# A two-stage convolution and scan kernel on one core: who adds up the sixteen units of the first level

## The chip, the cores and the metric

The kernel runs on one core of a Trainium2 chip. The metric is the device time of one execution in microseconds, where lower is better. A core has five engines with queues of their own: TensorE (PE in the profile; PEld is its weight load), VectorE (DVE), ScalarE (ACT), GpSimd (POOL) and SyncE (SP), which here issues every DMA. They meet only in semaphores. All data of the part in question are float32.

## The reference, cut to what matters

An input of 16 images with 256 channels of 32x32 goes through two residual blocks, each behind a group normalization. The first block computes 7x7 depthwise filters from the image and convolves the image with them. The second is a state-space scan over three levels of resolution (1024, 256 and 64 positions), in two directions:

```python
def _ssm(x, xw, dtw, dtb, Al, Dv, g, be):
    ...
    def step(h, inp):
        da, dbx, c = inp
        h = h * da + dbx
        return (h, jnp.einsum('bdn,bn->bd', h, c))
    ...
    y = ys.transpose(1, 0, 2) + xt * Dv
    return _layernorm(y, g, be)
```

So for each of 16 states n there is a scan over the positions, its result is multiplied by the row C[n], and the 16 products are summed. At the first level (1024 positions) this is done once forward and once backward. The sum plus x times D goes through a layer norm over the 128 channels, the two directions are added, and the result is gated, projected and added to the image.

## The kernel before

The 128 inner channels lie on the partitions, the positions along the free dimension. The scan of one image is cut into 37 *units* (`UNITS`): unit 0 is level 3, units 1 to 4 are level 2 (four states each, both directions), units 5 to 20 are the sixteen states of level 1 forward, and units 21 to 36 the sixteen of level 1 backward. A *product* (`PRODUCTS`) is one unit in one direction, so q = k + 5 for the units of level 1. For a unit k of level 1:

- SP fetches the broadcast rows B[n] into `bb` (two buffers, `get_b`) and C[n] into `cb` (three, `get_c`), 512 KB each. `get_b(k)` waits until `bx` of unit k-2 is made, `get_c(k)` until the products of unit k-3 are.
- GpSimd makes `bx` = `bb` * `u` (`inputs`, L1315; it needs the scan of unit k-2 done, since `bx` has two buffers). I call it bx(k).
- ScalarE makes the decay exp(delta * A[n]) in PSUM, `slot_b`, in two halves (`decay`, L1173), each after the scan of unit k-1 in the same half.
- VectorE scans each half (`scan`, L552) from `slot_b` and `bx` into PSUM, `slot_c`, the second half starting from the first one's last element, and multiplies each half by `cb` into SBUF, `h`, one of three buffers (`weigh`, L561). `products` orders this as: first scan of k, second multiply of k-1, second scan of k, first multiply of k. I call the start of a unit's first scan S(k).
- GpSimd adds the product `h` to the running sum `y` (`gather`, L1343). I call it y(k). Its program order is bx(k+1), y(k-1), bx(k+2), y(k), and so on, one unit ahead with the inputs and one behind with the sums.

The layer norm (`norm_centre` and `norm_spread` on TensorE, `norm_square` and `norm_root` on ScalarE, `norm` on VectorE) is done in six pieces (`NORMS`): 0 and 1 are levels 3 and 2, 2 and 3 the two halves of the forward direction, 4 and 5 those of the backward one. `norm_centre` multiplies `y` by the 128x128 matrix `cen`, which takes the mean over channels away.

Everything is software-pipelined over images. One *body* runs the 37 units of image i, the convolution of image i+1 (98 taps of six matmul instructions each; `taps`, L790), and the preparation of image i+2, interleaved by hand tables (`ROOM`, `pre`, `NORM_*`, `CHUNK_*`). TensorE's taps need `diag` matrices, which ScalarE makes between the decays (L1059). After unit 36 comes the *bridge*: it ends the norm and the output of image i (norms 4 and 5, `output`) and starts the scan of image i+1. A full body is run 14 times in a `Fori` loop; a body without preparation and one without taps end the program.

Other places that the prediction names: the first-level rows of B, C and delta are computed in *chunks* of 512 positions (`chunk` on TensorE, L831 and L832; `chunk_exp`, `chunk_log` on ScalarE; `chunk_first`, L500, and `chunk_last`, L508 and L510, on VectorE; `chunk_low` on GpSimd). Chunks 4 and 5 (backward direction) are done around units 13 to 16; chunk 4 starts on TensorE when norm 1 has ended on VectorE (L588). VectorE also adds the convolution to the image at units 10 and 33 (`conv_add`, L486); the second of these releases the statistics, the new weights and the rest of the body's end on ScalarE. VectorE's other small pieces of preparation (`pre`) lie at units 17 to 27, norms 2 and 3 at units 30 and 33. The buffer `ob` holds the output image from the bridge until its DMA has left, counted by `ob_free`.

Of the kernel before, what the change touches and what calls it, by code (L numbers as in the profile page):

```python
# [5 lines left out]
ALU = mybir.AluOpType  # L6
# [28 lines left out]
UNITS = [(3, 2, 2, 0, NS)] + [(2, 1, 2, n, 4) for n in range(0, NS, 4)] + \  # L35
# [3 lines left out]
PRODUCTS = [(u, d) for u, (_, _, dd, _, _) in enumerate(UNITS) for d in ((0, 1) if dd == 2 else (dd,))]  # L39
NP = len(PRODUCTS)  # L40
# [6 lines left out]
HR = 3  # L47
BR, CR = 2, 3
# [13 lines left out]
def banks(q):  # L62

    u, d = PRODUCTS[q]
    return (1, 0) if UNITS[u][0] == 1 and d else (0, 1)
# [7 lines left out]
def half_at(q, p):  # L73
    return 2 * (q - 2) + p
# [10 lines left out]

def weighed(q):
    return q + 1 if q < 2 else 2 * q


NHALF = 2 * (NP - 2)  # L90
# [3 lines left out]
def build(nc, a, bc, out):  # L94
    with ExitStack() as ctx:
        def sb(name, shape, dt=F32):
            return ctx.enter_context(nc.sbuf_tensor(name, shape, dt))

        def ps(name, shape, dt=F32):
            return ctx.enter_context(nc.psum_tensor(name, shape, dt))  # L100
# [32 lines left out]
        ident, cen, ones, grp, grp_m2, halves, halves_m2 = (mats[n] for n in CONSTS)  # L133
# [59 lines left out]
        u = sb("u", [P, LS])  # L193
        y = sb("y", [P, 2, LF])
        bb = sb("bb", [P, BR, HW])
        cb = sb("cb", [P, CR, HW])
# [11 lines left out]
        ob = sb("ob", [P, CT, HW])  # L208
# [3 lines left out]
        slot_c = ps("slot_c", [P, HW])  # L212
# [8 lines left out]
        ob_free = Count("ob_free", 16)  # L221
# [75 lines left out]
        q_h3 = Count("q_h3", 2)  # L297
        q_h = Count("q_h", NHALF)
        q_pr = Count("q_pr", weighed(NP - 1))
        q_y = Count("q_y", NP)  # L300
        n_y = Count("n_y", 24)
        n_yc = Count("n_yc", NN)
        n_sq = Count("n_sq", NN)
# [21 lines left out]
        def bank(t, k):  # L325
            return t[:, k * HALF:(k + 1) * HALF]

        def norm_psum(k):

            t = {4: slot_b, 5: slot_c}.get(k, pm)  # L330
            return bank(t, 0), bank(t, 1)
# [10 lines left out]
        def half(ap, b):  # L342
            return ap[:, b * HALF:(b + 1) * HALF]
# [5 lines left out]
        def _(sp):  # L349
# [29 lines left out]
            def get_c(i, k):  # L379
                if k >= CR:  # L380
                    sp.wait_ge(q_pr.sem, q_pr.at(i, weighed(products_of(k - CR)[-1])))
                get_rows(i, k, NS, cb[:, k % CR, :], c_in[k % CR])
# [34 lines left out]
        def _(dve):  # L417
# [137 lines left out]
            def weigh(i, q, p):  # L555
                k, b = PRODUCTS[q][0], banks(q)[p]
                dve.wait_ge(c_in[k % CR].sem, c_in[k % CR].at(i, 16 * (k // CR + 1)))
                dve.wait_ge(q_h.sem, q_h.at(i, half_at(q, p) + 1))
                if p == 0 and q >= HR:
                    dve.wait_ge(q_y.sem, q_y.at(i, q - HR + 1))  # L560
                nc.vector.tensor_tensor(half(h[:, q % HR], b), bank(slot_c, b), half(cb[:, k % CR], b), ALU.mult).then_inc(q_pr.sem, 1)  # L561

            def products(i, k):

                if k == 0:
                    weigh_least(i, 0)
                    weigh_least(i, 1)
                    return
                late = halves_of(k - 1)[-1] if k > 1 else None
                for q, p in halves_of(k):  # L570
                    same = late is not None and banks(late[0])[late[1]] == banks(q)[p]
                    if same:
                        weigh(i, *late)
                    scan(i, q, p)
                    if late is not None and not same:
                        weigh(i, *late)
                    late = q, p
                if k == NU - 1:
                    weigh(i, *late)
# [99 lines left out]
        def _(pe):  # L679
# [154 lines left out]
            def norm_centre(i, k):  # L834
                d, c0, n = NORMS[k]
                src = y[:, :, c0:c0 + n] if d == 2 else y[:, d, c0:c0 + n]
                cols = 2 * n if d == 2 else n
                if k == 0:
                    pe.wait_ge(y_init.sem, y_init.at(i, 5))
                elif k < 4:  # L840
                    pe.wait_ge(n_o.sem, n_o.at(i, STEPS[k]))
                pe.wait_ge(q_y.sem, q_y.at(i, NORM_NEEDS[k]))
                o = norm_psum(k)[0][:, 0:cols]
                if d == 2:
                    o = o.rearrange("p (d n) -> p d n", d=2)
                nc.tensor.matmul(o, cen[:, :], src, start=True, stop=True).then_inc(n_yc.sem, 1)  # L846

            def norm_spread(i, k):
                d, c0, n = NORMS[k]
# [10 lines left out]
            def bridge(i, j, m):  # L860
                def some(lo, hi):
                    if m is not None:
                        taps(m, BRIDGE_TAPS[lo], BRIDGE_TAPS[hi])
                some(2, 3)
                if j is not None:
                    lower(j, 0)
                some(3, 4)
                if j is not None:
                    lower(j, 1)
                some(4, 5)  # L870
                if j is not None:
                    chunk(j, 0)
                if i is not None:
                    norm_centre(i, 4)
                    norm_centre(i, 5)
                if j is not None:
                    chunk(j, 1)
                if i is not None:
                    norm_spread(i, 4)
                    norm_spread(i, 5)  # L880
                some(5, 6)
                if j is not None:
                    project_z(j)
                if i is not None:
                    output(i, 0)
                    output(i, 1)
                some(6, 7)
# [390 lines left out]
        def _(pool):  # L1278
# [43 lines left out]
            def gather(i, q):  # L1322

                k, d = PRODUCTS[q]
                lv, m = UNITS[k][0], UNITS[k][4]
                ln, fc, _, _ = LEVEL[lv]
                yv = y[:, d, fc:fc + ln]
                if q == 0:
                    pool.wait_ge(y_init.sem, y_init.at(i, 5))
                pool.wait_ge(q_pr.sem, q_pr.at(i, weighed(q)))  # L1330
                if m == 1:
                    src = h[:, q % HR, 0:ln]
                else:
                    g = ln + 1 if lv == 3 else ln
                    src = h[:, q % HR, 0:m * g].rearrange("p (m l) -> p m l", m=m)[:, :, 0:ln]
                while m > 1:
                    m //= 2
                    pool.tensor_tensor(src[:, 0:m], src[:, 0:m], src[:, m:2 * m], ALU.add).then_inc(n_y.sem, 1)  # L1338
                    gather.n += 1
                    pool.wait_ge(n_y.sem, n_y.at(i, gather.n))  # L1340
                if q:
                    pool.wait_ge(q_y.sem, q_y.at(i, q))
                pool.tensor_tensor(yv, yv, src[:, 0] if len(src.shape) == 3 else src, ALU.add).then_inc(q_y.sem, 1)  # L1343

            def bridge(i, j, m):
# [73 lines left out]
NORM_NEEDS = {0: 2, 1: 10, 2: 26, 3: 26, 4: 42, 5: 42}  # L1419
# [71 lines left out]
```

## Time and profile before

| | |
|---|---|
| median of 3 runs | 4224.79 us (4222.85 to 4224.82) |
| time of the profiled execution | 4222.54 us |
| its span, first to last instruction | 4220.7 us |
| around the span | 1.8 us |
| TensorE busy / VectorE / ScalarE / GpSimd | 3109.9 / 3209.0 / 2693.2 / 3290.3 us |
| first scan of the first image to that of the last | 257.66 to 3985.68 us: 15 bodies |
| one full body (first scans at 2006.17 and 2254.89 us) | 248.7 us |

A body takes 248.7 or 249.7 us in turn. The body from 2006 to 2255 us is the one that the rows show in detail. In a line of the timeline the first number is the start in us from the start of the span, the second the time that it covers, then engine, source line, operation, the tiles written and read with their shapes, how many instructions are merged, and in brackets how long the engine sat idle before and what ended that. Neighbouring instructions overlap by up to 0.1 us, so a printed length is a little more than the room that it takes. Source lines are those of the kernel before.

### The profile page before, as it was taken

How to read it: one execution, taken by the hardware profiler on the slowest of the kernel's cores; microseconds unless marked ns; L12 is line 12 of the kernel's file. 1: busy time of each engine (PE TensorE's matmuls, PEld its weight loads, DVE VectorE, ACT ScalarE, POOL GpSimd, SP SyncE). 2: the span in 40 equal slices, each digit the busy share in tenths (PEclk: the TensorE clock that was granted, in tenths of full speed). 3: DMA queues.
4: the chain of work that ended last, by engine and by line, in shares of the span. 5: the costliest groups of instructions: out<-in, count | busy, mean ns of one | idle time of the engine just before them, and what ended most of it. 6: DMA issues, size and time to landing. Idle time of an engine off the chain costs nothing.

```text
span 4220.7 us, 53011 instructions
## 1 busy us (share of the span) xinstructions
PE 3109.9 (74%) x12620; PEld 1400.2 (33%) x12620; DVE 3209.0 (76%) x3975; ACT 2693.2 (64%) x6662; POOL 3290.3 (78%) x1908
## 2 busy tenths in 40 slices
PE   6978777887777788777777877788787778877511
PEld 3433333333333333333333433333333333333200
DVE  1058788787877878787887878788787887878877
ACT  4467766666766666666656766665677666666532
POOL 0059698796968969697896969889696987969797
PEclk8989888998888899889898988999898889988755
DMA  1025455453545545354553544445354554635544
GB/s 41 1 101 195 147 163 169 157 205 127 186 150 166 186 136 204 134 178 152 170 201 122 199 149 165 161 168 203 119 195 145 167 170 157 204 118 192 163 165 167
DMA packets 187275, 664.08 MB, mean 157 GB/s; under 512 B 22736, under 2 KB 24672, under 8 KB 186976
## 3 DMA queue, kind: packets, MB, share of 16 engines
q1 hardware_dynamic: 186976, 661.47, 46.4%
q14 instruction: 280, 2.29, 0.2%
q8 instruction: 19, 0.31, 0.0%
HBM read 639.76 MB, written 21.63 MB: 157 GB/s over the span
## 4 chain that ended last, share of the span: by engine, by line
POOL 28%; issue 19%; ACT 16%; PE 14%; DVE 13%; DMA 7%; POOLq 1%; DVEq 1%; SPq 0%; ACTq 0%
POOL bx L1315 13%; POOL y L1343 7%; DMA bb<-bc_rows 7%; ACT diag L1059 7%; PE pconv L790 6%; POOL h L1338 5%; DVE h L561 4%; DVE slot_c L552 2%; POOL bx L1318 2%; DVE rs L508 2%; ACT slot_b L1173 2%; PE pm L832 1%; PE pm L807 1%; PE pm L831 1%; DVE rs L500 1%
## 5 line engine op out<-in xcount | busy, mean ns | idle before, releaser
L790 PE MATMUL pconv<-pad,diag 128*128 128x512 f16 x9408 | 2270.5, 398 | 314.3 <-ACT diag L1059 210.0
L790 PEld LDWEIGHTS pconv<-pad,diag 128*128 128x128 f16 x9408 | 932.0, 100 | 1618.0 <-issue 346.0
L1343 POOL TENSOR_TENSOR y<-y,h 128x1024 f32<-128x1024 f32 (+2 forms) x672 | 1324.5, 1971 | 162.9 <-DVE h L561 139.6
L1173 ACT ACTIVATE slot_b<-delta,nega 128x512 f32<-128x512 f32 (+1 forms) x1280 | 805.4, 639 | 951.3 <-DVE slot_c L552 911.6
L1315 POOL TENSOR_TENSOR bx<-bb,u 128x1024 f32<-128x1024 f32 x512 | 1220.1, 2383 | 31.9 <-DMA bb<-bc_rows 31.9
L552 DVE TENSOR_TENSOR_SCAN slot_c<-slot_b,bx 128x512 f32<-128x512 f32 (+1 forms) x1024 | 954.4, 956 | 315.6 <-POOL bx L1315 214.6
L561 DVE TENSOR_TENSOR h<-slot_c,cb 128x512 f32<-128x512 f32 x1280 | 860.6, 674 | 35.9 <-POOL y L1343 35.9
L552 DVE TENSOR_TENSOR_SCAN slot_c<-slot_b,slot_c,bx 128x512 f32<-128x512 f32 x512 | 663.6, 1296 | 74.5 <-ACT slot_b L1173 18.2
L1059 ACT ACTIVATE diag<-id,chi 128x128 f16<-128x128 f16 x1568 | 498.1, 387 | 10.3 <-PE pconv L790 9.6
L1059 ACT ACTIVATE diag<-id,clo 128x128 f16<-128x128 f16 x1568 | 496.4, 386 | 0.0
L1338 POOL TENSOR_TENSOR h<-h 128x512 f32<-128x512 f32 (+3 forms) x384 | 349.9, 911 | 20.9 <-DVE h L531 3.4
L1285 POOL TENSOR_TENSOR delta<-delta,rs 128x512 f32<-128x512 f32 (+1 forms) x96 | 97.7, 1017 | 324.6 <-DVE rs L510 324.6
L1318 POOL TENSOR_TENSOR bx<-bb,u 128x1024 f32<-128x1024 f32 x64 | 158.8, 2482 | 125.5 <-DMA bb<-bc_rows 97.9
L500 DVE SCALAR_TENSOR_TENSOR rs<-qs,es 128x512 f32<-128x512 f32 (+1 forms) x96 | 64.9, 676 | 223.6 <-ACT qs L1133 223.6
L831 PE MATMUL pm<-f,wbc 128*32 128x512 f32 (+1 forms) x192 | 102.3, 620 | 147.0 <-ACT delta L1129 74.2
L1295 POOL TENSOR_TENSOR f<-f,lnw 128x98 f32<-128x98 f32 x16 | 6.2, 388 | 182.8 <-ACT f L1003 182.8
L1139 ACT ACTIVATE qs<-qs 128x512 f32<-128x512 f32 (+1 forms) x96 | 50.5, 526 | 153.7 <-DVE rs L500 153.7
L852 PE MATMUL pm<-es,ones 128*128 128x512 f32 (+1 forms) x128 | 62.7, 573 | 113.2 <-ACT es L1183 113.2
L846 PE MATMUL pm<-y,cen 128*128 128x512 f32 (+1 forms) x128 | 60.3, 554 | 89.2 <-POOL y L1343 40.6
L722 PE MATMUL pm<-ident,xh 128*128 128x128 f32 x256 | 47.0, 343 | 98.3 <-ACT xg L1094 72.1
L832 PE MATMUL pm<-f,wdelta 128*128 128x512 f32 (+1 forms) x192 | 116.9, 698 | 0.0
L695 PE MATMUL pconv<-sg,grp 128*128 128x8 f32 x32 | 9.5, 371 | 145.5 <-DVE sg L431 145.5
(171 smaller groups left out, 3095.9 us busy)
## 6 DMA issues: line engine op xcount, KB each, us to landing
bb<-bc_rows SPq DMA_DIRECT2D x592, 512.0 KB, 4.4
cb<-bc_rows SPq DMA_DIRECT2D x592, 512.0 KB, 4.4
xr<-in_x SPq DMA_DIRECT2D x16, 1024.0 KB, 5.0
out<-ob SPq DMA_DIRECT2D x16, 1024.0 KB
bc_rows<-rows SPq DMA_DIRECT2D x64, 64.0 KB, 1.6
w<-in_w SPq DMA_DIRECT2D x2, 256.0 KB
wc<-in_wc SPq DMA_DIRECT2D x2, 256.0 KB
bc_rows<-rows SPq DMA_DIRECT2D x16, 32.0 KB, 4.0
```

Source lines behind the costliest of these rows:

```text
L500: nc.vector.scalar_tensor_tensor(er[:, k, 0:n], qs[:, k, 0:n], 1.0, es[:, k, 0:n], ALU.subtract, ALU.subtract).then_inc(ch_err.sem, 1)
L552: ins = nc.vector.tensor_tensor_scan(hv, av, bv, start, ALU.mult, ALU.add)
L561: nc.vector.tensor_tensor(half(h[:, q % HR], b), bank(slot_c, b), half(cb[:, k % CR], b), ALU.mult).then_inc(q_pr.sem, 1)
L790: ins = nc.tensor.matmul(bank(pconv, k), w, pad[:, t, part, rows:rows + 16, dx:dx + W], start=first and m == 0, stop=last and m == 2)
L831: nc.tensor.matmul(bank(pm, 0)[0:2 * NS, 0:n], wbc[:, st, :], f[:, fc:fc + n], start=True, stop=True).then_inc(ch_bc.sem, 1)
L832: nc.tensor.matmul(bank(pm, 1)[:, 0:n], wdelta[:, st, :], f[:, fc:fc + n], start=True, stop=True).then_inc(ch_dt.sem, 1)
L1059: ins = nc.scalar.activation(diag[:, r % RING, m, dx, :], id16[:, :], ACT.Copy, scale=(chi, clo)[m][:, t, dy * KK + dx:dy * KK + dx + 1])
L1173: ins = nc.scalar.activation(slot_b[:, o:o + w], delta[:, so + c:so + c + w], ACT.Exp, scale=nega[:, st, n0 + n:n0 + n + 1])
L1315: ins = pool.tensor_tensor(bx[:, k % 2, :], bb[:, k % BR, :], us, ALU.mult)
L1318: ins = pool.tensor_tensor(o, bb[:, k % BR, :].rearrange("p (m l) -> p m l", m=m), us[:, None, :].to_broadcast([P, m, ln]), ALU.mult)
L1338: pool.tensor_tensor(src[:, 0:m], src[:, 0:m], src[:, m:2 * m], ALU.add).then_inc(n_y.sem, 1)
L1343: pool.tensor_tensor(yv, yv, src[:, 0] if len(src.shape) == 3 else src, ALU.add).then_inc(q_y.sem, 1)
```

## The change

In each direction of level 1, three of the sixteen units are taken from GpSimd: those of the states 3, 8 and 13 (`OWN`), which are units 8, 13 and 18 forward and 24, 29 and 34 backward. VectorE sums their products in `ob`, which stands free between two images. The unit of state 3 writes its product straight to `ob` in place of `h`. Those of states 8 and 13 multiply in place in PSUM and then add the PSUM half to `ob`. GpSimd's `gather` returns at once for these units. `norm_centre` of pieces 2 to 5 does a second matmul with the same matrix on `ob`, accumulated in PSUM, so that the norm sees the sum of both. The count `q_y` of GpSimd's sums no longer counts the six units; `q_own` counts the in-place multiplies.

```diff
+OWN = (3, 8, 13)
+def own(q):
+    u, _ = PRODUCTS[q]
+    return UNITS[u][0] == 1 and UNITS[u][3] in OWN
+def added(q):
+    return sum(not own(v) for v in range(q))
+def kept(q):
+    return sum(own(v) and UNITS[PRODUCTS[v][0]][3] != OWN[0] for v in range(q))
...
-        q_y = Count("q_y", NP)
+        q_y = Count("q_y", added(NP))
+        q_own = Count("q_own", 2 * kept(NP))
... weigh
-                if p == 0 and q >= HR:
-                    dve.wait_ge(q_y.sem, q_y.at(i, q - HR + 1))
+                if own(q):
+                    part, total = bank(slot_c, b), half(ob[:, PRODUCTS[q][1]], b)
+                    if UNITS[k][3] == OWN[0]:
+                        if p == 0:
+                            dve.wait_ge(ob_free.sem, ob_free.at(i + 1, 0))
+                        nc.vector.tensor_tensor(total, part, half(cb[:, k % CR], b), ALU.mult).then_inc(q_pr.sem, 1)
+                        return
+                    dve.wait_ge(q_h.sem, q_h.at(i, half_at(q, 1) + 1))
+                    nc.vector.tensor_tensor(part, part, half(cb[:, k % CR], b), ALU.mult).then_inc(q_own.sem, 1)
+                    dve.wait_ge(q_own.sem, q_own.at(i, 2 * kept(q) + p + 1))
+                    nc.vector.tensor_tensor(total, part, total, ALU.add).then_inc(q_pr.sem, 1)
+                    return
+                if p == 0 and q >= HR and not own(q - HR):
+                    dve.wait_ge(q_y.sem, q_y.at(i, added(q - HR + 1)))
... norm_centre
-                pe.wait_ge(q_y.sem, q_y.at(i, NORM_NEEDS[k]))
+                pe.wait_ge(q_y.sem, q_y.at(i, added(NORM_NEEDS[k])))
...
-                nc.tensor.matmul(o, cen[:, :], src, start=True, stop=True).then_inc(n_yc.sem, 1)
+                    nc.tensor.matmul(o, cen[:, :], src, start=True, stop=True).then_inc(n_yc.sem, 1)
+                    return
+                last = max(v for v in range(NP) if own(v) and PRODUCTS[v][1] == d)
+                pe.wait_ge(q_pr.sem, q_pr.at(i, weighed(last)))
+                nc.tensor.matmul(o, cen[:, :], src, start=True, stop=False)
+                nc.tensor.matmul(o, cen[:, :], ob[:, d, c0:c0 + n], start=False, stop=True).then_inc(n_yc.sem, 1)
... gather
+                if own(q):
+                    return
...
-                    pool.wait_ge(q_y.sem, q_y.at(i, q))
+                    pool.wait_ge(q_y.sem, q_y.at(i, added(q)))
```

## Rows read from the trace of the kernel before

**Rows 1.** The page: busy time of each engine, share of the span and instructions.
```profile
PE 3109.9 (74%) x12620; PEld 1400.2 (33%) x12620; DVE 3209.0 (76%) x3975; ACT 2693.2 (64%) x6662; POOL 3290.3 (78%) x1908
```

**Rows 2.** The page's costliest group on GpSimd: busy us, mean ns, idle before and releaser.
```profile
L1343 POOL TENSOR_TENSOR y<-y,h 128x1024 f32<-128x1024 f32 (+2 forms) x672 | 1324.5, 1971 | 162.9 <-DVE h L561 139.6
```

**Rows 3.** Busy time by window: us, PE, PEld, DVE, ACT, POOL busy, clock, DMA.
```profile
2128.00:2207.00 79.00, 65.64 (x314) 33.12 (x314) 68.18 (x84) 46.75 (x110) 78.92 (x38) 0.94 0.63 220
```

**Rows 4.** Timeline of GpSimd: bx of unit 20 and y of unit 18.
```profile
2137.42 2.36 POOL L1315 TENSOR_TENSOR bx<-bb,u 128x1024 f32<-128x1024 f32 x1
...
2139.74 2.35 POOL L1343 TENSOR_TENSOR y<-y,h 128x1024 f32<-128x1024 f32 x1
```

**Rows 5.** Timeline of VectorE: the first scans of units 32 and 33.
```profile
2197.55 1.23 DVE L552 TENSOR_TENSOR_SCAN slot_c<-slot_b,bx 128x512 f32<-128x512 f32 x1
...
2201.40 1.23 DVE L552 TENSOR_TENSOR_SCAN slot_c<-slot_b,bx 128x512 f32<-128x512 f32 x1
```

**Rows 6.** Timeline of GpSimd, ScalarE and VectorE around the sum of unit 8.
```profile
2083.35 2.37 POOL L1343 TENSOR_TENSOR y<-y,h 128x1024 f32<-128x1024 f32 x1
...
2083.31 0.68 ACT L1173 ACTIVATE slot_b<-delta,nega 128x512 f32<-128x512 f32 x1
...
2084.19 1.23 DVE L552 TENSOR_TENSOR_SCAN slot_c<-slot_b,bx 128x512 f32<-128x512 f32 x1 [1.48 <-ACT slot_b L1173]
```

**Rows 7.** Busy time by window, VectorE alone: us, busy, clock, DMA share, GB/s.
```profile
2084.00:2108.00 24.00, 22.39 (x29) 0.95 0.58 184
```

**Rows 8.** Timeline from norm 1 on VectorE to chunk 4 on TensorE and back.
```profile
2103.61 0.49 DVE L588 TENSOR_TENSOR o<-pm,o 128x128 f32<-128x128 f32 x2
...
2104.15 1.05 PE L831 MATMUL pm<-f,wbc 128*32 128x512 f32 x2 [3.75 <-DVE o L588]
...
2109.35 0.69 DVE L500 SCALAR_TENSOR_TENSOR rs<-qs,es 128x512 f32<-128x512 f32 x1 [1.14 <-ACT qs L1133]
```

**Rows 9.** Single source lines on VectorE: count, duration in ns min/median/max, first and last start.
```profile
L561 DVE TENSOR_TENSOR h<-slot_c,cb x1280: 664/673/693, 270.4 to 4196.9; 128x512 f32<-128x512 f32 x183
...
L603 DVE TENSOR_TENSOR slot_b<-slot_b,delta x16: 699/700/700, 495.5 to 4206.6; 128x512 f32<-128x512 f32 x16
...
L510 DVE TENSOR_TENSOR rs<-rs,es x96: 224/691/2731, 247.7 to 4101.2; 128x512 f32<-128x512 f32 x64, 128x64 f32<-128x64 f32 x16, 128x256 f32<-128x256 f32 x16
```

**Rows 10.** Timeline of VectorE: two steps of norm 2, the second waiting for the first.
```profile
2191.07 0.69 DVE L603 TENSOR_TENSOR pm<-pm,rs 128x512 f32<-128x512 f32 x1
...
2191.79 0.82 DVE L613 TENSOR_SCALAR pm<-pm,vec,bes 128x512 f32<-128x512 f32 x1
```

**Rows 11.** Waits by kind from 2128 to 2207 us: total us, times, longest.
```profile
DVE slot_c L552 <- POOL bx L1315: 5.6, 9, 0.8
```

**Rows 12.** Timeline: bx of unit 27 on GpSimd, first scan of unit 27 on VectorE.
```profile
2170.63 2.36 POOL L1315 TENSOR_TENSOR bx<-bb,u 128x1024 f32<-128x1024 f32 x1
...
2173.11 1.23 DVE L552 TENSOR_TENSOR_SCAN slot_c<-slot_b,bx 128x512 f32<-128x512 f32 x1 [1.62 <-ACT slot_b L1173]
```

**Rows 13.** Timeline: second conv_add on VectorE, TensorE after its last taps, GpSimd's sum of unit 33.
```profile
2207.59 1.28 DVE L486 SCALAR_TENSOR_TENSOR xn<-pconv,csc,xn 128x1024 f32<-128x1024 f32 x1
...
2211.44 0.59 PE L695 MATMUL pconv<-sg,grp 128*128 128x8 f32 x2 [9.42 <-DVE sg L431]
...
2213.25 2.36 POOL L1343 TENSOR_TENSOR y<-y,h 128x1024 f32<-128x1024 f32 x1 [2.95 <-DVE h L561]
```

**Rows 14.** Timeline of TensorE in the bridge, and of ScalarE after it.
```profile
2238.16 1.02 PE L846 MATMUL slot_c<-y,cen 128*128 128x512 f32 x2
...
2249.40 1.88 PE L857 MATMUL slot_b<-o,wo 128*128 128x512 f32 x4
...
2253.82 1.67 ACT L1173 ACTIVATE slot_b<-delta,nega 128x256 f32<-128x256 f32 x4 [2.74 <-DVE ob L628]
```

**Rows 15.** View of the tile bb: from issue of its DMAs to landing.
```profile
DMA to landing us min/median/max: 3.3/4.4/8.0
```

**Rows 16.** Timeline of TensorE: norm 4 at the end of the last image.
```profile
4200.06 2.08 PE L846 MATMUL slot_b<-y,cen 128*128 128x512 f32 x2 [22.92 <-POOL y L1343]
```

## The prediction

> **What bounds the kernel now.** I read the page first. GpSimd is the busiest engine and VectorE close behind [rows 1], but both are averages over stretches with different limits. GpSimd's costliest group is the one that the change cuts [rows 2]. So the question is where GpSimd is what the next step waits for. For that I went through the timelines of one full body, engine by engine, and looked at which engine has no gaps.
>
> There are three kinds of stretch. From 2128 to 2207 us (units 18 to 33) GpSimd works 78.92 of 79 us and VectorE 68.18 [rows 3]: GpSimd is the bound. A unit costs it bx and y at 2.32 us each [rows 4], 4.63 in all, where VectorE needs 3.85 for a plain unit when nothing holds it up [rows 5]. The reader should see that VectorE has only 0.78 us to spare per unit, and that its preparation work and the norms come out of that. From 2084 to 2108 us (units 10 to 14) VectorE is busy 22.39 of 24 us [rows 7]: it is the bound there, although GpSimd is full too. From 2207 us to the first units of the next image neither matters: ScalarE, then TensorE, then ScalarE again run without gaps, and GpSimd waits.
>
> **The change, part by part, for one full body.**
>
> *Unit 8, y gone, product written to `ob`.* VectorE's work is the same. GpSimd is free at 2083.35 instead of 2085.7. Nobody is waiting for it: the scan of unit 10 waits 1.48 us for a decay that ScalarE starts only at 2083.31 [rows 6], and then VectorE is the bound to 2108. Gain 0. If GpSimd were what unit 10 waited for, it would be up to 2.3. The wait on `ob_free` is for a DMA of the bridge, some 70 us old; 0.
>
> *Unit 13, y gone, VectorE adds.* The y saved is again worth 0. Before, a half cost one multiply, 0.67 us. Now it costs an in-place PSUM multiply like L603's, 0.70, and an add of PSUM and SBUF operands like L561's, 0.67 to 0.69 [rows 9]. A step that waits for the one just before starts 0.72 after it [rows 10], where independent ones overlap by 0.1. And the first half's multiply now waits for the second scan to end instead of overlapping it. I take 0.88 more for the first half and 0.72 for the second, 1.6 per unit. The bounds: 1.4 (two bare adds) and 2.2 (0.2 more for each of the four new waits). Norm 1 comes right behind the first half, on the engine that is the bound. When it ends, at 2104.1, TensorE starts chunk 4, for which it has been waiting 3.75 us, and VectorE in turn waits 1.14 for that chunk [rows 8]. So 0.88 goes on the path; the second half's 0.72 falls into the 1.14. Everything to unit 18 is 0.9 later. Cost 0.9.
>
> *Units 18, 24 and 29 in the stretch that GpSimd bounds.* GpSimd loses three y, 3 x 2.32 = 7.0 us. VectorE gets 2 x 1.6 = 3.2 us more (unit 24 costs it nothing). So VectorE must make up what is saved, and can only give what it waited for. The waits for bx in this window are 5.6 us in 9 pieces [rows 11], of which 0.3 lies before unit 18. To them comes 1.62 at unit 27, which the profile puts down to ScalarE, but bx(27) ends at 2172.99 and the scan starts at 2173.11 [rows 12]. That is 6.9 us. I walked the units with the durations above: bx(21) starts 2.3 earlier, but units 19 to 22 use up VectorE's waits on unit 18's adds and its own preparation (S(20) and S(21) are 0.8 late, S(22) even); then VectorE runs without waiting and S(24) and S(25) are 0.8 and 1.6 early. At unit 26 GpSimd is late once more by some 0.7, since y(19) had to wait for its product; y(24) then cures that. S(27) is 3.3 early, S(29) 3.7. Unit 29's adds eat 0.88 and 0.72, of which unit 30 gives back 0.8. S(33) is 2.9 to 3.0 early: 6.9 - 0.7 - 3.2 = 3.0. Bounds: 3.7 if unit 26 doesn't wait either, 0.7 if the relief of one y (2.3) is lost on the way. TensorE doesn't stop it: its last taps end 9.42 before 2211.44, thus at 2202.0, and conv_add at 2207.6 doesn't wait [rows 13]; it has 5.6 us of room, and the second centre matmul of norms 2 and 3 takes 1.8 of it. Gain 3.0, which reaches conv_add of unit 33 and through it the whole end of the body.
>
> *Unit 34.* y(33) waits 2.95 us for VectorE already [rows 13], so one y less is worth 0. The 1.6 more on VectorE lie beside ScalarE's gapless chain. 0; without that cover 1.6.
>
> *The second centre matmul in the bridge.* A float32 matmul of 128x512 is two instructions and takes 0.9 us (1.02 printed, less the overlap) [rows 14]. Norms 4 and 5 get one each, 1.8 us. They lie where TensorE goes from chunk 0 through norms 4 and 5, chunk 1 and the gate's projection to the output at 2249.40 without a gap, and ScalarE waits 2.74 us for what VectorE makes of the output [rows 14]; from there ScalarE sets the start of the next image. So it counts in full. Cost 1.8; bounds 0.9, if half of it hid behind ScalarE's squares, and 1.8.
>
> *Waits by queue.* `get_c(k)` on SP now waits 1.6 longer behind units 18 and 29. `get_b` of the next unit stands behind it, but waits longer anyway for its bx. Fewer than 3 us are added to a load that is needed two units later: 0.
>
> Sum for a full body: 0.9 - 3.0 + 1.8 = -0.3, times 14 = -4. The body without preparation: VectorE has more waits to give, but is the bound from unit 30 on; I get about 0. The last one: chunk 4's wait is long enough to take the 0.9, the sum of 18 to 30 gives 2.7, but units 29 and 34 now add 1.6 + 0.7 on VectorE after that, and the two matmuls come at the end at TensorE's low clock first (2.08 for what takes 1.02) [rows 16], 1.8 to 3: about +1. In all -3 us on the profiled 4222.5, which stands 2.3 below the median of the three runs. Against the median that is 4221.8; I say 4221.5.
>
> **A rule that speaks against it.** VectorE's L510, with both operands in SBUF, takes 0.69 us as a rule and 2.73 at worst, beside GpSimd; L561, with one operand in PSUM, never leaves 0.664 to 0.693 in 1280 times, GpSimd working nearly always [rows 9]. The new adds are of the second kind. The Trainium skill (Perfetto Trace Analysis, Optimizing Scalar/DVE Operations) warns that GpSimd and VectorE share an SBUF read port, so that moving work between them might not help. Taken at its word, the adds and GpSimd would block each other; that is rival 2. The Trainium skill's page SBUF — State Buffer (SBUF: two separate sides) limits this to VectorE operations in a two-port mode or with two SBUF inputs, and by that limit the price is 0.
>
> **The rivals.**
> 1. *Faster: the relief comes through.* If unit 26 doesn't wait (0.7) and half of the bridge's matmuls hides (0.9), a body gains 1.9: 14 x 1.9 + 2 = 29, so 4196. If unit 13's 0.9 is hidden too, 4183. For it: GpSimd has no gap over 79 us. Against it: VectorE has 6.9 us and no more. Chance 0.34.
> 2. *Slower: the adds and GpSimd block each other.* An add at the mean of L510's two ends is 1.7, 1.0 more. Five adds a body lie on the path: +5, so 14 x 5 = 70, 4292. It decides from 0.2 us per add on. L561 speaks against it. Chance 0.04.
> 3. *Slower: the stretch doesn't speed up.* bx has only two buffers and `get_b(k)` starts at the end of bx(k-2). Without the y between, the row is wanted 4.6 us after that; it lands after 4.4 at the median, 8.0 at most [rows 15]. At the median it is in time, and VectorE has 1.5 us of work in hand. If loads or the preparation chain (TensorE's transposes and products, ScalarE's weights) eat the saving whole, a body costs 0.9 + 1.8 = 2.7 more: +38, 4262. With 1.2 of the 3.0 lost a body is 0.9 slower, and it is measurably slower. Chance 0.20.
> 4. *My forecast*, 4213 to 4230: 0.42.
>
> **How the numbers follow.** A measurement of this kernel tells 0.2%, 8.4 us, from no change. The forecast's own range is 0.6 us per body either way, 4213 to 4230, and lies in "same" but for its ends: same 0.41. Faster is rival 1 and a bit of the forecast's lower end, 0.36; slower is rivals 2 and 3, 0.23. The range to leave out 2 in 10: down past rival 1's first time, and up to where half of rival 3 (1.5 us per body, +21) lies: 4193 to 4245.
>
> **What would show it.** In a full body after: y at L1343 x576, GpSimd some 220 us less busy; VectorE some 90 us more. The new adds at 0.67 to 0.70 us. No VectorE wait for bx to speak of between units 22 and 33; S(33) to S(19) 63 us instead of 66.1. Norm 1 to chunk 4 unchanged in length, 0.9 later. In the bridge TensorE 1.8 longer without a gap. I am wrong if VectorE still waits for bx in that stretch, if the adds take over 0.9, or if the bridge doesn't grow.

## The result and the profile after

The changed kernel takes 4282.23 us in the median of four runs (4273.1 to 4284.99), the kernel before 4223.82 (4221.43 to 4224.82): ratio 1.0135, 95% interval 1.0118 to 1.0153. It is 58 us slower, and 37 us above the end of my range. The profiled execution took 4273.1 us with a span of 4271.3, at the low end of the four, so what follows explains 51 of the 58.

The page of the kernel after, against [rows 1] and [rows 2]:

```profile
PE 3184.0 (75%) x12748; PEld 1440.8 (34%) x12748; DVE 3340.5 (78%) x4103; ACT 2697.7 (63%) x6662; POOL 3065.8 (72%) x1812
...
L1382 POOL TENSOR_TENSOR y<-y,h 128x1024 f32<-128x1024 f32 (+2 forms) x576 | 1097.8, 1906 | 334.0 <-DVE h L593 311.1
```

GpSimd does what was asked: 96 sums fewer, 224.5 us less busy. VectorE is 131.5 us busier, where I had said some 90. The groups of VectorE's instructions by form say what the rest is (in the kernel after the scan is L572, the multiply into `h` L593, the in-place multiply L587, the add to `ob` L589, dg L474, the bound of wsc L497):

```profile
L589 DVE TENSOR_TENSOR ob<-slot_c,ob 128x512 f32<-128x512 f32 x128 | 88.5, 692 | 4.4
L587 DVE TENSOR_TENSOR slot_c<-slot_c,cb 128x512 f32<-128x512 f32 x128 | 87.8, 686 | 3.0
...
L497 DVE TENSOR_SCALAR wsc<-sa 128x2 f32<-128x2 f32 x16 | 29.8, 1865 | 0.5
L474 DVE TENSOR_SCALAR dg<-ident,sk 49x49 f32<-49x49 f32 x16 | 19.3, 1205 | 0.6
...
L482 DVE COPY fi<-pm 128x98 f32<-128x98 f32 x16 | 4.2, 260 | 50.6 <-PE pm L770 50.6
```

The adds cost what I had said, 692 ns each, and the new adds and multiplies less the old multiplies are 90.6 of the 131.5 us. But two small preparation instructions that the change doesn't touch have grown, by 31.9 us together: dg, 49x49 elements, from 9.5 to 19.3 us, and wsc, two elements per partition, from 7.7 to 29.8. dg is a diagonal matrix; TensorE multiplies it into kt, VectorE copies kt out, TensorE makes fi from it, and VectorE copies fi out. wsc is the largest absolute weight of each channel's new filter, kept above 1e-30. The copy of fi now waits 50.6 us for TensorE. The kernel before had these rows, which my prediction doesn't use (there dg is L454 and wsc L477; min/median/max in ns):

```profile
L454 DVE TENSOR_SCALAR dg<-ident,sk x16: 241/647/657, 37.1 to 3634.5; 49x49 f32<-49x49 f32 x16
...
L477 DVE TENSOR_SCALAR wsc<-sa x16: 168/526/535, 60.9 to 3672.4; 128x2 f32<-128x2 f32 x16
```

and after:

```profile
L474 DVE TENSOR_SCALAR dg<-ident,sk x16: 241/1182/2382, 36.1 to 3679.9; 49x49 f32<-49x49 f32 x16
...
L497 DVE TENSOR_SCALAR wsc<-sa x16: 169/2130/2134, 58.2 to 3716.2; 128x2 f32<-128x2 f32 x16
```

For the places I took the start of the first scan of each unit, counted from the start of its body, as the mean of the second to the fourteenth full body, and formed the lengths between them. The last column is VectorE's mean wait for fi over the 14 bodies with preparation. The table holds all kernels of this study, which are told below:

```
us per body    to S(13)  13-18  18-22  22-27  27-31  31-36  36-end   body   mean wait for fi
before            92.01  33.09  18.65  23.81  20.58  31.52   29.80  249.46   0.46
after             91.57  34.15  22.01  20.12  22.29  31.52   31.40  253.06   2.70
e1_mm             91.58  32.77  18.80  23.68  20.58  31.51   31.92  250.84   0.81
e2_dg_act         91.54  34.20  19.58  20.27  22.28  31.51   31.40  250.78   1.65
e3_no18           91.67  33.93  19.60  21.29  22.31  31.87   31.82  252.49   1.75
e4_early          91.88  33.94  22.51  19.95  22.30  31.52   29.70  251.80   3.21
e5_wsc            91.88  33.88  22.45  20.05  20.75  31.52   31.52  252.05   3.18
e6_before_both    91.84  33.10  18.51  23.95  20.58  31.50   30.06  249.54   0.20
e7_all            91.50  34.36  19.45  20.10  20.70  31.52   30.51  248.14   1.53
e8_all_no13       91.54  33.05  20.94  20.07  20.75  31.51   30.31  248.17   2.57
e9_all_8_only     91.68  32.95  18.74  22.14  20.70  31.51   29.91  247.63   0.70
e10_tap           91.58  33.07  18.72  20.97  20.88  31.51   30.10  246.83   0.40
e11_before_tap    92.01  32.94  18.51  23.97  20.58  31.51   29.68  249.20   0.21
```

After against before, a body gains 0.44 up to unit 13, loses 1.06 to unit 18, loses 3.36 to unit 22, gains 3.69 to unit 27, loses 1.71 to unit 31, and loses 1.60 in the bridge: 3.60 slower. The relief of GpSimd is there, in units 22 to 27. It is lost on both sides of them.

**The loss at units 27 to 31.** The timelines of VectorE and of GpSimd in the body that begins at 2025.09 us:

```profile
2194.10 0.24 DVE L496 TENSOR_REDUCE sa<-wg 128x2 f32<-128x98 f32 x1
2194.37 2.13 DVE L497 TENSOR_SCALAR wsc<-sa 128x2 f32<-128x2 f32 x1
2196.54 0.17 DVE L498 RECIPROCAL sa<-wsc 128x2 f32<-128x2 f32 x1
...
2194.12 2.36 POOL L1382 TENSOR_TENSOR y<-y,h 128x1024 f32<-128x1024 f32 x1
```

wsc ends at 2196.50, when y ends (2196.48). The tensor_reduce before it and the reciprocal behind it are as small and are not held: in the kernel before they run inside a GpSimd operation that goes on behind them, in all 14 bodies, and take 0.24 and 0.17 us. In all 14 bodies with preparation wsc ends 0.02 to 0.03 us behind the GpSimd operation that was running when it started. It was so in the kernel before as well, but there it started 1.86 us into GpSimd's operation and lasted 0.53; now it starts 0.24 to 0.42 into one and lasts 2.13 to 1.97. dg shows the same: before it starts 1.75 into an operation of 2.36 and lasts 0.65; after, in the six bodies in which GpSimd stands idle at that moment, it takes 0.24, and in the eight others 2.12 to 2.38, ending 0.04 to 0.05 behind GpSimd's operation. Such an operation waits for the end of GpSimd's: in the thirteen traces dg or wsc started on VectorE beside a running GpSimd operation 154 times, and each time it ended 0.02 to 0.05 us behind that operation's end. The relief has moved GpSimd's operations against VectorE's. So these two engines do not meet only in semaphores, as I wrote of all five at the start.

The Trainium skill has both halves of this: SBUF — State Buffer (SBUF: two separate sides) states that of a GpSimd operation and a VectorE operation in a two-port mode the one that starts first holds the shared pair for its whole length, and VectorE: DVE Perf Modes (Mode 2×_2P — use both read ports for one tensor) that a float32 tensor_scalar from SBUF to SBUF runs in that mode and a tensor_tensor doesn't. The durations above agree. My prediction cited the first, held it against the new adds alone, and did not look for old operations of this kind.

**The loss at units 18 to 22.** TensorE and VectorE in the next body, 2275.60 to 2530.53 us (kt is L762, made with dg; L770 makes fi out of kt; L822 are the taps between them):

```profile
2409.61 1.54 PE L822 MATMUL pconv<-pad,diag 128*128 128x512 f16 x6
2413.62 3.05 PE L762 MATMUL pm<-dg,ex 49*128 49x49 f32 x16 [2.47 <-DVE dg L474]
2416.60 5.01 PE L822 MATMUL pconv<-pad,diag 128*128 128x512 f16 x12
2421.44 2.77 PE L770 MATMUL pm<-kt,xg 128*128 128x49 f32 x24
...
2411.18 2.38 DVE L474 TENSOR_SCALAR dg<-ident,sk 49x49 f32<-49x49 f32 x1
2413.48 1.21 DVE L572 TENSOR_TENSOR_SCAN slot_c<-slot_b,bx 128x512 f32<-128x512 f32 x1
...
2425.15 0.26 DVE L482 COPY fi<-pm 128x98 f32<-128x98 f32 x1 [3.62 <-PE pm L770]
```

The same stretch in the kernel before:

```profile
2132.84 7.12 PE L790 MATMUL pconv<-pad,diag 128*128 128x512 f16 x24
2139.89 1.98 PE L730 MATMUL pm<-dg,ex 49*128 49x49 f32 x16
2141.80 2.85 PE L790 MATMUL pconv<-pad,diag 128*128 128x512 f16 x12
2144.49 3.67 PE L738 MATMUL pm<-kt,xg 128*128 128x49 f32 x32
...
2139.18 0.65 DVE L454 TENSOR_SCALAR dg<-ident,sk 49x49 f32<-49x49 f32 x1
...
2148.19 0.26 DVE L462 COPY fi<-pm 128x98 f32<-128x98 f32 x1 [0.23 <-PE pm L738]
```

TensorE now stands idle 2.47 us for dg, and the twelve taps behind take 5.01 us for what took 2.85. The granted clock of the two stretches, after and before (columns: window, length, busy us of PE, PEld, DVE, ACT and POOL, clock, DMA share, GB/s):

```profile
2415.00:2425.00 10.00, 10.00 (x53) 6.86 (x54) 6.33 (x8) 6.65 (x18) 9.29 (x4) 0.69 0.61 211
```

```profile
2139.90:2149.00 9.10, 9.10 (x66) 7.08 (x66) 8.12 (x10) 5.83 (x16) 9.10 (x5) 1.00 0.66 236
```

1.00 is the level of 2.4 GHz all through; 0.69 is a stretch of which most lay at 1.2 GHz, behind an idle TensorE. VectorE waits 2.70 us per body for fi instead of 0.46, and all of its scans stand behind that copy.

### The profile page after: what moved, and what is told of

It reads as the page before. It is cut to its first block, busy times and chain, and to the rows that moved or that the text cites. A ratio compares the mean times of both kernels' runs of the same rounds, so it can differ in the third digit from the quotient of the medians.

```text
span 4271.3 us, 53179 instructions
## 1 busy us (share of the span) xinstructions
PE 3184.0 (75%) x12748; PEld 1440.8 (34%) x12748; DVE 3340.5 (78%) x4103; ACT 2697.7 (63%) x6662; POOL 3065.8 (72%) x1812
## 4 chain that ended last, share of the span: by engine, by line
DVE 23%; ACT 22%; issue 21%; PE 19%; POOL 13%; DVEq 1%; POOLq 0%; SPq 0%; DMA 0%; ACTq 0%
ACT diag L1096 10%; PE pconv L822 8%; DVE h L593 7%; POOL bx L1352 6%; DVE slot_c L572 5%; POOL h L1377 3%; ACT slot_b L1210 3%; POOL bx L1355 2%; PE pm L864 2%; DVE rs L528 1%; POOL y L1382 1%; PE pm L863 1%; PE pm L770 1%; DVE slot_c L587 1%; DVE ob L589 1%
## 5 line engine op out<-in xcount | busy, mean ns | idle before, releaser
L822 PE MATMUL pconv<-pad,diag 128*128 128x512 f16 x9408 | 2273.1, 398 | 316.7 <-ACT diag L1096 211.7
L822 PEld LDWEIGHTS pconv<-pad,diag 128*128 128x128 f16 x9408 | 932.3, 101 | 1624.1 <-issue 347.6
L1382 POOL TENSOR_TENSOR y<-y,h 128x1024 f32<-128x1024 f32 (+2 forms) x576 | 1097.8, 1906 | 334.0 <-DVE h L593 311.1
L1352 POOL TENSOR_TENSOR bx<-bb,u 128x1024 f32<-128x1024 f32 x512 | 1204.5, 2355 | 99.6 <-DMA bb<-bc_rows 98.8
L572 DVE TENSOR_TENSOR_SCAN slot_c<-slot_b,bx 128x512 f32<-128x512 f32 (+1 forms) x1024 | 954.3, 956 | 190.5 <-POOL bx L1352 131.9
L593 DVE TENSOR_TENSOR h<-slot_c,cb 128x512 f32<-128x512 f32 x1088 | 731.8, 674 | 35.8 <-POOL y L1382 35.8
L572 DVE TENSOR_TENSOR_SCAN slot_c<-slot_b,slot_c,bx 128x512 f32<-128x512 f32 x512 | 663.8, 1296 | 74.5 <-ACT slot_b L1210 16.4
L1355 POOL TENSOR_TENSOR bx<-bb,u 128x1024 f32<-128x1024 f32 x64 | 160.6, 2509 | 117.4 <-DMA bb<-bc_rows 89.1
L528 DVE TENSOR_TENSOR rs<-qs,rs 128x512 f32<-128x512 f32 (+1 forms) x96 | 77.7, 809 | 44.7 <-ACT qs L1176 44.7
```

What stands on the lines that cost most here:

```text
L528: nc.vector.tensor_tensor(er[:, k, 0:n], qs[:, k, 0:n], er[:, k, 0:n], ALU.subtract).then_inc(ch_sub.sem, 1)
L572: ins = nc.vector.tensor_tensor_scan(hv, av, bv, start, ALU.mult, ALU.add)
L822: ins = nc.tensor.matmul(bank(pconv, k), w, pad[:, t, part, rows:rows + 16, dx:dx + W], start=first and m == 0, stop=last and m == 2)
L1352: ins = pool.tensor_tensor(bx[:, k % 2, :], bb[:, k % BR, :], us, ALU.mult)
L1355: ins = pool.tensor_tensor(o, bb[:, k % BR, :].rearrange("p (m l) -> p m l", m=m), us[:, None, :].to_broadcast([P, m, ln]), ALU.mult)
```

## The experiments

**e1_mm: the second centre matmuls alone.** In the kernel before:

```diff
+                if k >= 2:
+                    nc.tensor.matmul(o, cen[:, :], src, start=True, stop=True)
                 nc.tensor.matmul(o, cen[:, :], src, start=True, stop=True).then_inc(n_yc.sem, 1)
```

The norm's output is unchanged, since the second matmul overwrites the first.

> The kernel before, with the centre matmul of norms 2 to 5 done twice on the same operand, the first result overwritten. Nothing is moved between engines. If the bridge price is as counted (1.7 us per image, all on the path, the two matmuls of norms 2 and 3 hidden), 4224 + 16 x 1.75 = 4252. If norms 2 and 3 also count, up to 4280; if the bridge hides them, 4224.

4247.34 us (4243.71 to 4249.32), ratio 1.0054 (1.0037 to 1.0070): 24 us. The bridge is 2.1 longer, 31.92, and units 27 to 36, where the second matmuls of norms 2 and 3 lie, are as long as before. The term of 1.8 stands, and it is some 24 of the 58 us.

**e2_dg_act: dg's scaling on ScalarE.** In the changed kernel:

```diff
-                nc.vector.tensor_scalar(dg49[:, :], ident[0:K2, 0:K2], sk[:, 2:3], None, ALU.mult).then_inc(a_dg.sem, 1)
+            def a_dgs_(j):
+                act.wait_ge(dve_a.count.sem, dve_a.count.at(j, 1))
+                nc.scalar.activation(dg49[:, :], ident[0:K2, 0:K2], ACT.Copy, scale=sk[:, 2:3]).then_inc(a_dg.sem, 1)
```

ScalarE does it in unit 19.

> The changed kernel with the 49x49 scaling that makes dg (L474) on ScalarE instead of VectorE, which has nothing to do there. If the 2.1 to 2.4 us that it took in half of the bodies is VectorE waiting for GpSimd, and the late copy of fi follows from it, those bodies fall from 255 to the 250.5 of the others: 4282 - 8 x 4.5 = 4246. If only the late start after unit 18's adds matters (TensorE idle, then at a lower clock), it stays within 10 us of 4282.

4246.36 us (4242.22 to 4250.51), ratio 1.0055 (1.0038 to 1.0072): 36 us came back, as the lock theory had said. The wait for fi falls from 2.70 to 1.65, units 18 to 22 from 22.01 to 19.58. wsc is still held:

```profile
2182.30 2.13 DVE L496 TENSOR_SCALAR wsc<-sa 128x2 f32<-128x2 f32 x1
```

**e3_no18: unit 18 given back to GpSimd.** `OWN` lists the units themselves, 8, 13 forward and 24, 29, 34 backward; 8 and 24 write straight to `ob`.

> The changed kernel with unit 18 given back to GpSimd: VectorE sums units 8, 13, 24, 29 and 34. If unit 18's adds, which stand ahead of dg, are what costs the 2.0 and 5.6 us per body that the prediction missed, VectorE's wait for fi falls back from 50.6 to about 20 us, dg to 0.65, and a body to 249 to 250: 4230 to 4240, though one y less is taken from GpSimd. If the cause is elsewhere (the other adds, the matmuls), giving back work to the engine that bounds makes it slower or the same: 4280 to 4300.

4272.87 us (4269.57 to 4274.83), ratio 1.0116 (1.0099 to 1.0133). Units 18 to 22 are 2.41 shorter than in the changed kernel, but units 22 to 27, without the relief of y(18), are 1.17 longer, and 9 us come back where I had expected 42 to 52. So unit 18's adds are a part of the loss there and not all of it. dg is back at 0.65 us in every body and no later than in the kernel before (8.81 us from the second transposes to kt in both), and yet VectorE waits 1.75 us for fi in the mean:

```profile
2153.09 6.24 PE L823 MATMUL pconv<-pad,diag 128*128 128x512 f16 x24
2160.13 2.44 PE L763 MATMUL pm<-dg,ex 49*128 49x49 f32 x16 [0.81 <-DVE dg L475]
2162.51 5.30 PE L823 MATMUL pconv<-pad,diag 128*128 128x512 f16 x12
```

Here the 24 taps ran sooner at the full clock (6.24 us where the kernel before shows 7.12), TensorE had 0.81 us to stand, and the low clock fell on kt and the taps behind it. So the wait for fi has a cause of its own beside the lock: TensorE has nothing to do just before kt. That is argued here from one stretch, and e10_tap tests it. wsc still takes 2.12 to 2.15 us in every body.

**e4_early: the second matmuls of norms 4 and 5 where TensorE waits.** In the changed kernel `norm_centre` of pieces 4 and 5 is split:

```diff
+            def norm_own(i):
+                pe.wait_ge(q_pr.sem, q_pr.at(i, weighed(NP - 1)))
+                for k in (4, 5):
+                    d, c0, n = NORMS[k]
+                    nc.tensor.matmul(norm_psum(k)[0][:, 0:n], cen[:, :], ob[:, d, c0:c0 + n], start=True, stop=False)
...
                 some(2, 3)
+                if i is not None:
+                    norm_own(i)
                 if j is not None:
                     lower(j, 0)
```

> The changed kernel with the matmuls on ob of norms 4 and 5 issued before the first lowering, where TensorE waits 1.83 us for ScalarE. If the 1.72 us that the bridge grew are these matmuls and TensorE is what it waits for, the bridge shrinks by 1.7 and the time by 14 x 1.7 + 2 = 26: 4256. If the growth comes from something else in the bridge, 4282.

4252.41 us (4239.4 to 4256.63), ratio 1.0056 (1.0036 to 1.0076): 30 us came back, and the bridge is 29.70, as before the change. The profiled execution is the slowest of its four and that of the changed kernel the fastest, so the two are only 16 us apart: the body is 1.26 shorter, since the bridge gives 1.70 and the wait for fi takes 0.5.

**e5_wsc: no small tensor_scalar at unit 27.** In the changed kernel `wg` gets one more column, which holds 1e-30, and the reduce bounds wsc by itself:

```diff
-                ch(nc.vector.tensor_reduce(s[:, 80:82], wg[:, :, :], AX.X, ALU.max, apply_absolute_value=True))
-                ch(nc.vector.tensor_scalar(wsc[:, :], s[:, 80:82], 1e-30, None, ALU.max))
+                ch(nc.vector.tensor_reduce(wsc[:, :], wgx[:, :, :], AX.X, ALU.max, apply_absolute_value=True))
```

> The changed kernel, with VectorE's 128x2 tensor_scalar that bounds wsc from below (1.87 us mean in the changed kernel, 0.48 before) left out: the bound stands as a column of 1e-30 beside the weights, and the tensor_reduce writes wsc itself. Nothing of the result changes. Theory A (this small SBUF to SBUF operation stands behind a running GpSimd addition and the delay passes on to the end of the body): the body loses 1.5 us or more, 16 times: 4282 - 24 = about 4258, and the 128x98 tensor_reduce stays at its old duration. Theory B (the delay at unit 27 is slack, since VectorE waits later for GpSimd's or ScalarE's work): within 3 us of 4282. Theory C (the lock passes on to the next SBUF-only operation there, the reduce or the reciprocal): that operation then shows 2.1 us and the time stays at 4275 to 4282.

4258.22 us (4246.27 to 4261.38), ratio 1.0077 (1.0058 to 1.0096): 24 us came back, theory A. Units 27 to 31 take 20.75 instead of 22.29; the wait for fi is 0.48 longer. The reduce and the reciprocal are not held:

```profile
L498 DVE TENSOR_REDUCE wsc<-wgx 128x2 f32<-128x100 f32 x16 | 3.9, 245 | 26.5 <-ACT wgx L1050 26.5
...
L499 DVE RECIPROCAL sa<-wsc 128x2 f32<-128x2 f32 x16 | 2.7, 166 | 0.5
```

**e6_before_both: the kernel before with the edits of e2 and e5.**

> The kernel before, with both small SBUF to SBUF operations taken off VectorE: dg's scaling (0.65 us) on ScalarE, wsc's bound in the reduce (0.48 us). Nothing of the result changes. If the two cost the kernel before only what their own rows show, it gains at most 1.1 us a body, less what dg loses by a start on ScalarE: 4223 - 10 = 4213, bounds 4205 and 4223. If instead the two were as dear before as in the changed kernel, it would gain over 30 us, to about 4190.

4222.33 us (4220.11 to 4225.29), ratio 1.0001 (0.9991 to 1.0011). No gain, where I had expected 10 us. The two operations cost the kernel before nothing; they became dear with the change.

**e7_all: the changed kernel with the edits of e2, e4 and e5.**

> The changed kernel with dg's scaling on ScalarE, wsc's bound in the reduce, and the second centre matmuls of the last two pieces issued ahead of the lower part, where TensorE waits. If the three losses are separate and add up: 4282 - 36 - 24 - 30 = 4192. If dg's and wsc's delays hide one behind the other, or the clock of TensorE keeps half of it: about 4210.

4207.38 us (4204.47 to 4209.75), ratio 0.9967 (0.9954 to 0.9979): 75 us below the changed kernel, where the three alone bring 90. The 15 us between are not located, and they are not seen in the profiled executions, which lie 30, 16 and 12 us below the changed kernel's for the three alone and 69 for all. What is left of the losses is 1.3 at unit 13, 0.7 in the bridge and a wait for fi of 1.53 instead of 0.46. With these the change makes the kernel faster.

**e8_all_no13: unit 13 back to GpSimd as well.**

```diff
-OWN = (3, 8, 13)
+OWN = (8, 18, 24, 29, 34)
+FIRST = (8, 24)
```

> The one before it, with unit 13 given back to GpSimd: own units 8 (first), 18 forward and 24 (first), 29, 34 backward. Unit 13's two adds cost S(14) 0.4 to 0.8 us, which my prediction took as 0.9. If GpSimd has room for unit 13's product (it waits for rows of VectorE there): 0.8 us a body below the one before it, 12 us: about 4180. If the addition takes GpSimd's lead in the units after it away: the same as the one before it, or up to 10 us above.

4196.72 us (4193.37 to 4201.34), ratio 0.9938 (0.9921 to 0.9954). Units 13 to 18 are 1.31 shorter, and 1.5 of that is given back in units 18 to 22, where the wait for fi rises to 2.57. The bodies of the two profiles are equal (248.14 and 248.17), and the profiled executions 3 us apart; the 11 us between the medians are not located.

**e9_all_8_only: unit 18 back too.** Own units 8 (first), and 24 (first), 29, 34.

> The best so far (dg's scaling on ScalarE, wsc's bound in the reduce, the last two pieces' second matmuls early, GpSimd adds unit 13's product) with unit 18's product given back to GpSimd as well: VectorE sums unit 8 (first) forward and 24 (first), 29, 34 backward. If unit 18's adds cost dg's start 0.8 us and so TensorE's clock (12 taps 4.07 to 5.30 us behind it against 2.85), and GpSimd's lead there does not need the relief: VectorE's wait before fi falls from 2.5 us to the 0.2 to 0.4 us of the kernel before: 4197 - 30 = 4167. If TensorE's clock in that stretch goes by something other than how late dg is (in the run without unit 18's adds, with dg on VectorE, the wait was 1.85 to 3.43 us in ten of fourteen bodies): 4190 to 4200. If GpSimd's lead is lost: above 4200.

4197.12 us (4195.6 to 4197.72), ratio 0.9939 (0.9922 to 0.9956), the same as e8 and 30 above what I had expected, and in the range that I had given to another cause. The wait for fi falls to 0.70, and units 18 to 22 are 2.2 shorter. But GpSimd has y(18) again and is late in units 22 to 27, which are 2.07 longer. VectorE's waits for bx, in e8 and here:

```profile
DVE slot_c L573 <- POOL bx L1368: 139.3, 91, 4.1
```

```profile
DVE slot_c L573 <- POOL bx L1368: 210.0, 190, 4.1
```

So unit 18's relief is worth 2 us a body, and its adds cost as much through fi.

**e10_tap: e8 with one tap moved ahead of kt.** Six matmuls of unit 20 are issued in unit 19:

```diff
     n = min(n, PREP)
-    return BRIDGE_TAPS[-1] + ...
+    return (n == 20) + BRIDGE_TAPS[-1] + ...
```

> The best so far with the six matmuls of one tap issued in unit 19 ahead of the kt matmuls instead of in unit 20 between them and the fi matmuls. TensorE stands idle 0.49 to 1.54 us before kt there; the six take 1.4 us at the full clock. Theory A (the wait of VectorE for fi, 2.5 us in the mean, comes of that idle time and the lower clock granted behind it, and of twelve matmuls that stand before fi): the idle time goes, six matmuls less stand before fi, the wait falls under 0.5 us and the time to 4197 - 28 = about 4168. Theory B (the lower clock falls into this stretch whatever TensorE does before kt): the six matmuls less before fi still save 1.4 to 2.6 us a body if kt does not come later, 4160 to 4175, but the rows of the six matmuls left behind kt then show over 2 us instead of 1.4. If the six go past dg's start at the low clock, kt is later by up to 1 us: 4185.

4180.88 us (4179.02 to 4182.5), ratio 0.9900 (0.9884 to 0.9917). In e8 this body read:

```profile
2376.38 2.43 PE L763 MATMUL pm<-dg,ex 49*128 49x49 f32 x16 [1.11 <-ACT dg L1148]
2378.74 5.30 PE L823 MATMUL pconv<-pad,diag 128*128 128x512 f16 x12
```

and here, with VectorE's copy:

```profile
2359.77 7.88 PE L823 MATMUL pconv<-pad,diag 128*128 128x512 f16 x30
2367.59 1.98 PE L763 MATMUL pm<-dg,ex 49*128 49x49 f32 x16
2369.50 1.55 PE L823 MATMUL pconv<-pad,diag 128*128 128x512 f16 x6
2372.04 3.21 PE L771 MATMUL pm<-kt,xg 128*128 128x49 f32 x27 [0.98 <-DVE kt L480]
...
2375.84 0.26 DVE L484 COPY fi<-pm 128x98 f32<-128x98 f32 x1 [0.16 <-PE pm L771]
```

TensorE arrives at kt without having stood (at most 0.21 us in any body), and the six matmuls behind it take 1.55 us, the full clock, in all 14 bodies. The granted clock is 1.00 from 2367.6 to 2375.9 us; in e8 it is 0.66 from 2376 to 2386. Theory A. The wait falls by 2.2 us and the body by 1.3, since 0.9 comes back in units 22 to 27 (20.97 against 20.07). Hence 16 us of the expected 28.

**e11_before_tap: the same three edits in the kernel before.**

> Control for the one before it: the kernel before with the same three edits that are not the change (dg on ScalarE, wsc's bound in the reduce, one tap ahead of kt). VectorE waits for fi 0.16 to 0.40 us there without the tap's move, so the move can bring at most 0.2 us a body: 4222 - 3 = 4219, within 0.2% of the kernel before; if the tap makes kt late, up to 4230.

4221.08 us (4217.4 to 4223.49), ratio 0.9995 (0.9985 to 1.0004): nothing, as expected. So the 40 us between e11 and e10 are the change's own, once unit 13 is left out and what it disturbs is put right.

## Why the prediction was wrong, by its own steps

- *Unit 8, gain 0*: 0.44 was gained up to unit 13, small and on the good side.
- *Unit 13, cost 0.9*: units 13 to 18 are 1.06 longer. Right, and the adds at 692 and 686 ns too; in the body at 2025 us S(14) and the start of chunk 4 are 0.88 and 0.89 later behind S(13) than before, as worked out.
- *Units 18 to 33, gain 3.0*: **this step failed**; the stretch is 1.4 us longer than before (72.12 against 70.74 from S(18) to S(33)). Of its parts, units 22 to 27 gained 3.69 where I had walked to 3.3. Units 18 to 22 were to come out even and lost 3.36: 2.24 of it is the wait for fi, the rest unit 18's adds and dg behind GpSimd. After unit 27 0.3 was to be lost, and it was 1.71, of which e5 gives back 1.54 by taking wsc away. Without dg's scaling and wsc on VectorE (e7) the stretch takes 67.95, that is 2.8 below before: the movable waits were summed rightly. What failed is two terms put at nothing. I took the preparation's small instructions at their old durations, where wsc costs 1.54 and dg, with what hangs on it, 2.28 (e2's body against the changed kernel's). And for "TensorE doesn't stop it" I looked at its last taps and not at kt and fi, where VectorE waits 2.24 longer, a part of it through dg. So a body came out at +3.60 instead of the -0.3 of my sum.
- *Unit 34, 0*: units 31 to 36 are 31.52 before and after. Right.
- *The bridge, 1.8*: 1.60 in the changed kernel, 2.1 in e1_mm. Right in kind and size. That it was avoidable, e4 shows.
- *SP's queue, 0*: the landing of bb is 4.5 us at the median, 4.4 before [rows 15]. bx now waits more for bb, 98.8 us in all against 31.9, 93 of it at units 14 and 15, but VectorE waits 132.1 us for bx against 214.6, and in the chain that ended last bb is 0% of the span against 7%. Right.
- *The sum*: the first full body is as long as before (249.4), 13 x 3.60 = 46.8 come from the others, 4.06 from the body without preparation, 0.5 from what lies before the first scan, and -0.8 from the last image: 50.6, the difference of the two spans. For the two at the end I had 0 and +1. That body without preparation takes 238.7 to 238.8 us against 235.55 in e6_before_both and e11_before_tap too, which have no adds, so the 4.06 can't be put down to the adds alone; why is open.

Of the rivals, the second had the right mechanism at the wrong place: it put GpSimd's port against the new adds, which read PSUM and stayed at 692 ns, and gave it 0.04. The third had the place, a preparation chain that eats the saving whole, TensorE's products among it, at 4262; it named neither the lock nor TensorE's idle time and clock, and the measured 4282 is 20 above it. Of what I said would show me wrong, no point came true: VectorE hardly waits for bx in units 22 to 33 of the body at 2025 us, no add takes 0.9, the bridge grew. The list lacked the length of the instructions that the change only moves. S(19) to S(33), which the prediction writes the other way round, is 67.4 in the mean instead of the 63 that I gave (66.1 before), and that line alone showed it.

The clue stood in rows of before: dg took 0.65 us for 49x49 elements in 14 bodies, ending each time as GpSimd's operation ended, and 0.24 ahead of them, where GpSimd had no work yet. The upper bound for both is one whole operation of GpSimd, 2.36 us: 1.7 and 1.8 more than they took, 3.5 a body, 50 us in all, and it belonged in the range.

What stays open: which idle times of TensorE bring the low clock to the stretch behind kt. In the thirteen traces the taps behind kt are slow in one of the 68 bodies in which TensorE stood under 0.3 us before kt, and in 93 of the 114 with 0.3 us or more (twelve taps each, six in e10_tap and e11_before_tap). But within these the length doesn't decide: in e2_dg_act the taps behind 1.5 us of idle took 2.85 us and those behind 0.4 took 4.46. What does decide there, no run shows.

## What to carry to other kernels

When a change shifts one engine of a pair in which one can wait for the other's whole instruction, as VectorE's float32 tensor_scalar from SBUF to SBUF did for GpSimd's here, list the old instructions of that kind on the other engine, small ones too, and price each at a full operation of the first. When an engine's waits are to be made up elsewhere, ask of every engine in the chain what it will stand idle for; here TensorE's idle time ahead of kt cost up to 4.1 us behind it (kt 3.65 instead of 1.98, the twelve taps 5.30 instead of 2.85). And an offload that measures slower may still be worth having: here five edits around it turned +1.4% into -1.0%, and three of them bring nothing to the kernel before.

## What the runs showed of the hardware

- A float32 tensor_scalar on VectorE with both sides in SBUF stands until a running GpSimd tensor_tensor ends, however small it is: 128x2 elements took 0.17 us alone and up to 2.15 beside one, 49x49 took 0.24 and up to 2.38. A tensor_reduce (0.24), a reciprocal (0.17), a copy out of PSUM (0.26) and a tensor_tensor with one operand in PSUM (0.69) beside the same GpSimd operations did not.
- TensorE's twelve 128x512 float16 matmuls between kt and fi took 2.85 us at the granted clock of 1.00, and 4.1 to 5.3 in 93 of the 114 bodies in which TensorE had stood idle for 0.3 us or more before kt. VectorE's wait for fi came in steps accordingly: at most 0.40 us with the twelve at 2.85, and never under 1.5 with them at 4.0 or more.
